# Cross attention and a routed feed-forward block: the transposition of the inputs ahead of the scores, the scaled block product ahead of the final sum

## The chip, the cores and the metric

The kernel runs on one core of one Trainium2 chip. The metric is the device time of one execution in microseconds, as the median of several runs.

## What is computed

The reference, cut to what matters (B = 128 items, T = 128 tokens each, E = 256, H = 16 heads of D = 16, all float32):

```python
x = x + xattn(layernorm(x), ctx)          # Wq, Wkv, Wo, biases
x = x + ffn(layernorm(x))                 # w_router, w_block

def xattn(inp, enc):
    q, k, v = inp @ Wq + bq, enc @ Wk + bk, enc @ Wv + bv     # 16 heads of 16
    scores = einsum('bhqd,bhkd->bhqk', q, k) / sqrt(D)
    attn = softmax(scores, axis=2)        # over the queries
    return einsum('bhqk,bhkd->bhqd', attn, v) @ Wo + bo

def ffn(x):
    top = top_k(x @ w_router, k=96)       # of the 128 tokens of an item
    return x.at[top].set(gelu(x[top] @ w_block))
```

## The kernel before

Each of the five engines runs its own program, written out by hand, and semaphores order them. An item b is one of the 128; the work is a pipeline in which a loop over **slots** `s` runs one stage each for different items. In slot s TensorE makes the scores of item s, transposes the inputs of item s + 5, makes the values of item s - 1, the keys or the queries of a later pair, the projection of item s - 2, the block product (the feed-forward matmul and the router's score) of item s - 4, the transposition of the attention's result of item s - 3, and the attention of item s - 1.

The code below is the program of TensorE for a slot (lines 524 to 541); `settled` or `sure` leaves out waits that the order makes needless:

```python
scores(s)
transpose_inputs(s + 5, s > 2)
values(s - 1)
queries_or_keys(s + 2, 1, sure)
queries_or_keys(s + 3, 0, sure)
...
```

What matters for the change:

- `scores` (line 336, matmuls in line 349) uses the array in four row tiles: 32 rows by 128 columns each. It waits for `recip_23_ready` and `exp_ready[1]` of the item before, which free its PSUM banks.
- `transpose_inputs` (line 361, matmuls in line 378) transposes two halves of `xhat` (the normalised x) and two of `c_sb` (the context) into the bank `ps_t`, with the whole array. From item 10 on it waits for `z_ready` of item b - 10, since `ps_t` also holds the block product: VectorE's `product_scaled` (line 860, operation in line 870) reads that product out of it and raises `z_ready`. So in slot s the transposition waits for the product that VectorE scales in slot s - 1.
- `attention` (line 401, matmuls in line 414) uses the array in four column tiles: 128 rows by 32 columns. It waits for `x1_ready`, which `residual` (line 767, operation in line 773) raises.
- ScalarE takes 16 exponentials with their sums for each item (`exps`, line 593), and between them casts and copies, among them `inputs_high` (line 606), which reads the transposed inputs, and `gelu_tanh` (line 637).
- VectorE's slot (lines 960 to 995) is: `x1_low` (764), four maxima (751) of which the first two wait for the scores, `values_and_bias` (858), `inputs_low` (819), `inverse_sums_01` (811), the queries (832) or the keys (845), `residual` (773), the last maximum, `inverse_sums_23` (804), `final` (923), the statistics of a pair (780 or 797), and `product_scaled` (870). Between them stand the steps of `router`, which finds the 32 dropped tokens of each item for eight items at once. They are spread over slots with s mod 8 of 4, 5, 6, 7 and 0, from s = 12 on. After the third maximum, step 10 (906 and 907) comes where s mod 8 is 0 and step 0 (885) where it is 4. A `max` (896) stands just ahead of `inverse_sums_23` where s mod 8 is 4, 5, 6 or 7. Step 9 (901) comes after the second maximum where s mod 8 is 0.
- GpSimd normalises, scales the values, and does half of the gelu. SyncE issues the DMAs.

An fp32 matmul has two records in the trace, so the 8 matmuls of the scores are 16 rows, the 4 transpositions are 4 rows.

Of the kernel before, what the change touches and what calls it, by code (L numbers as in the profile page):

```python
# [6 lines left out]
def cross_attention_routed_ffn(  # L7
# [40 lines left out]
    with ctx:  # L48
# [81 lines left out]
        def bank(b, j):  # L130
            return J if j == 0 and b % 2 == 1 else j

        def inputs_bank(b):
            return ps_a if b in (1, 3) else ps_t
# [7 lines left out]
        def has(b):  # L142
            return 0 <= b < B

        def upto(b):
            return min(b + 1, B)

        def pair(b):
            return b % R // 2

        def landed(b):
            return b // R * 16 + 16
# [136 lines left out]
        def _(pe):  # L289
# [29 lines left out]
            def pair_ready(b, settled=False):  # L319

                if b % 2 == 0 and has(b):
                    if b == 0:
                        pe.wait_ge(q_raw_ready, upto(b + 1))
                    else:
                        pe.wait_ge(q_eo_in[(b // 2) % 2], stripes(b))
                    if not settled:
                        pe.wait_ge(k_ready, upto(b + 1))

            def inputs_ready(b):

                if has(b):
                    pe.wait_ge(xhat_ready, upto(b))
                    if b % 2 == 0:
                        pe.wait_ge(c_in[pair(b)], landed(b))

            def scores(b):

                if not has(b):
                    return
                r2, h = (b // 2) % 2, b % 2  # L340
                if b == 0:
                    pair_ready(b)
                if has(b - 1):
                    pe.wait_ge(recip_23_ready, upto(b - 1))
                    pe.wait_ge(exp_ready[1], upto(b - 1))
                for c in range(C):
                    for j in range(J):
                        rows = slice(32 * j, 32 * j + 32)
                        mm = nc.tensor.matmul(ps_s[:, bank(b, j), c, :, :], k_sb[rows, r2, c, h * T:(h + 1) * T],  # L349
                                              q_eo[rows, r2, :, c, h, :], start=True, stop=True)  # L350
                        if c == C - 1:
                            mm.then_inc(s_mm[j], 1)
# [8 lines left out]
            def transpose_inputs(b, settled=False):  # L361

                if not has(b):
                    return
                if not settled:
                    inputs_ready(b)
                if has(b - 10):
                    pe.wait_ge(z_ready, upto(b - 10))
                elif 2 <= b <= 4:
                    pe.wait_ge(t_lo_ready, upto(b - 2))  # L370
                elif b > 4:
                    pe.wait_ge(t_lo_ready, upto(b - 1))
                for kind in range(2):
                    for c in range(C):
                        src = (xhat[:, b % 4, c * P:(c + 1) * P] if kind == 0
                               else c_sb[:, b % 8, c * P:(c + 1) * P])
                        n = kind * C + c
                        mm = nc.tensor.transpose(inputs_bank(b)[:, n * T:(n + 1) * T], src, ident[:, :])  # L378
                mm.then_inc(t_mm, 1)
# [17 lines left out]
            def scaled_values_ready(b):  # L397

                pe.wait_ge(v_pad_ready, upto(b))
# [20 lines left out]
            def values(b):  # L420

                if not has(b):
                    return
                if b == 0:
                    pe.wait_ge(w_lo_ready["v"], 1)
                    pe.wait_ge(w_z_ready, 1)
                if b == B - 1:
                    pe.wait_ge(x1_ready, upto(b - 2))
                elif has(b - 1):
                    pe.wait_ge(o_ready, upto(b - 1))  # L430
                n, h = (b // 2) % 4, b % 2
                three_terms(ps_v,
                            lambda a, c: (t_hi, t_lo)[a][:, n, 1, c, h * T:(h + 1) * T],
                            lambda a, c: (w_hi, w_lo)[a]["v"][:, c, :]).then_inc(v_mm, 1)
# [88 lines left out]

            for s in range(2, B - 1):
                sure = 20 <= s < B - 8
                scores(s)
                transpose_inputs(s + 5, s > 2)
                values(s - 1)
                queries_or_keys(s + 2, 1, sure)
                queries_or_keys(s + 3, 0, sure)  # L530
                keep_columns(s - 16)
                candidates(s - 12)
                projection(s - 2, sure)
                pair_ready(s + 1, sure)
                inputs_ready(s + 6)
                block_product(s - 4, sure)
                if sure:
                    scaled_values_ready(s - 1)
                transpose_x1(s - 3, sure)
                router_bank_free(s + 1)  # L540
                attention(s - 1, sure)
# [175 lines left out]
        def _(dve):  # L717
# [82 lines left out]
            def inverse_sums_23(b):  # L800

                if has(b):
                    dve.wait_ge(exp_ready[2], upto(b))
                    nc.vector.reciprocal(recip[:, b % 4, :].rearrange("p (c j q) -> p j c q", c=C, j=J)[:, 2:4, :, :],
                                         ps_s[:, 2:4, :, :, 0]).then_inc(recip_23_ready, 1)
# [54 lines left out]
            def product_scaled(b, settled=False):  # L860

                if has(b):
                    dve.wait_ge(z_mm, upto(b))
                    if not settled:
                        dve.wait_ge(rstd2_ready, upto(b))
                    if b % 2 == 0 and has(b - R):
                        dve.wait_ge(stored[pair(b)], landed(b - R))
                    if b == 0:
                        dve.wait_ge(w_lo_ready["v"], 1)
                    nc.vector.tensor_scalar(z_sb[:, b % R, :], ps_z, rstd2[:, b % R:b % R + 1], None,  # L870
                                            ALU.mult).then_inc(z_ready, 1)
# [37 lines left out]
            def final(b, settled=False):  # L909

                if has(b):
                    if b in U_ON_ACT:
                        dve.wait_ge(u_act_ready, u_on_act(b))
                    else:
                        dve.wait_ge(u_ready, b + 1 - u_on_act(b))
                    if settled:
                        pass
                    elif b < GELU_ON_DVE:
                        dve.wait_ge(gelu_ready, upto(b))
                    else:  # L920
                        dve.wait_ge(gelu_dve_ready, b - GELU_ON_DVE + 1)
                    k, r = b % GROUP, b % R
                    nc.vector.scalar_tensor_tensor(z_sb[:, r, 0:E], z_sb[:, r, 0:E], half_keep[:, (b // GROUP) % 2, k:k + 1],  # L923
                                                   x1_sb[:, r, :], ALU.mult, ALU.add).then_inc(final_ready, 1)
# [35 lines left out]
            for s in range(2, B):  # L960
                sure = 20 <= s < B - 1
                x1_low(s - 4)
                if s == 3:
                    block_weights_low()
                router(s - 13, 2)
                router(s - 14, 4)
                router(s - 15, 6)
                router(s - 16, 8)
                maxima(s, 3)
                maxima(s, 2)  # L970
                router(s - 16, 9)
                values_and_bias(s - 1, sure)
                inputs_low(s + 5)
                inverse_sums_01(s - 1)
                maxima(s, 1)
                queries(s + 3, sure)
                router(s - 16, 10)
                router(s - 12, 0)
                keys(s + 2, sure)
                residual(s - 2, sure)  # L980
                maxima(s, 0)
                if s == B - 1:
                    values_and_bias(B - 1)
                router(s - 12, 1)
                router(s - 13, 3)
                router(s - 14, 5)
                router(s - 15, 7)
                inverse_sums_23(s)
                final(s - 16, sure)
                stats2_of_pair(s - 3)  # L990
                if s >= 4:
                    stats1_of_pair(s + 10)
                product_scaled(s - 4, sure)
                if s < 4:
                    stats1_of_pair(2 * s + 6)

# [258 lines left out]
```

## Time and profile before

| | before |
|---|---|
| median of 3 runs | 900.6 us (900.34 to 901.68) |
| profiled execution, its own time | 898.87 us |
| its span | 897.1 us |
| PE, PEld busy | 97%, 84% |
| DVE, ACT, POOL busy | 95%, 97%, 89% |
| granted TensorE clock, mean | 0.991 |

PE is TensorE's matmuls, PEld its weight loads, DVE is VectorE, ACT ScalarE, POOL GpSimd. The times of matmul ends are modelled. An instruction of ACT that stands in the engine's queue behind another is counted as busy from its issue, so that the duration of one holds its time in the queue. "[0.33 <-DVE z_sb L870]" behind a row says how long the engine was idle before it and what the profile holds to have released it; "issue" means that it shows no releaser.

### The profile page before, as it was taken

To read this page: it belongs to the slowest core of one execution; us is meant where nothing else is said; L and a number is where in the kernel's file an instruction comes from. 1 tells how busy PE (TensorE), PEld (TensorE's weight loads), DVE (VectorE), ACT (ScalarE), POOL (GpSimd) and SP (SyncE) were. 2 spreads that over 40 slices of the span, in tenths; PEclk is the share of its full clock that TensorE was granted. 3 is DMA by queue.
4 is the path that set the end of the run, shared out by engine and by line. 5 is a ranking of instruction groups with operands and counts; after the bars stand their busy time and mean duration, and the time that the engine had idled before them with its cause. 6 is when DMAs were issued, how large, how long until landed. Compare 5 with 4: busy or idle time off the path is not lost. (4 is left out here: it accounts for less than half of the span.)

```text
span 897.1 us, 31627 instructions
## 1 busy us (share of the span) xinstructions
PE 867.0 (97%) x10562; PEld 757.0 (84%) x10562; DVE 852.6 (95%) x2068; ACT 869.5 (97%) x4632; POOL 794.4 (89%) x1488
## 2 busy tenths in 40 slices
PE   7999999999999999999999999999999999999972
PEld 6788888888888888888888888888888888888862
DVE  6898999999999999999999999999999999999987
ACT  5999999999999999999999999999999999999984
POOL 4668889999999999999999999999999999998764
PEclk9999999999999999999999999999999999999996
DMA  6222123233233223233223223323322322311102
GB/s 204 64 65 73 47 63 96 57 88 95 58 88 95 66 83 93 61 88 92 76 74 92 74 77 90 91 61 88 84 69 88 96 59 85 97 46 52 49 25 94
DMA packets 70978, 70.48 MB, mean 79 GB/s; under 512 B 12064, under 2 KB 62752, under 8 KB 70816
## 3 DMA queue, kind: packets, MB, share of 16 engines
q1 hardware_dynamic: 69456, 67.68, 26.3%
q8 instruction: 84, 1.38, 0.6%
q10 hardware_dynamic: 1360, 0.79, 0.3%
q14 instruction: 78, 0.64, 0.2%
HBM read 35.13 MB, written 16.78 MB: 58 GB/s over the span
## 5 line engine op out<-in xcount | busy, mean ns | idle before, releaser
L593 ACT ACTIVATE e_sb<-ps_s,neg_max 128x128 f32<-128x128 f32 x2048 | 776.7, 661 | 2.4 <-DVE neg_max L751 2.1
L593 ACT ACTIVATION_READ_ACCUMULATOR e_sb<-ps_s,neg_max 128x1 f32 x2048 | 735.0, 486 | 0.0
L751 DVE TENSOR_REDUCE neg_max<-ps_s 128x4 f32<-128x512 f32 x512 | 331.7, 668 | 24.0 <-PE ps_s L349 22.5
L349 PE MATMUL ps_s<-q_eo,k_sb 32*128 32x256 f32 x2048 | 146.7, 400 | 1.4 <-ACT e_sb L593 0.6
L414 PE MATMUL ps_a<-e_sb,v_pad 128*32 128x128 f32 x4096 | 138.3, 276 | 2.1 <-POOL v_pad L1086 0.9
L310 PE MATMUL ps_a<-w_o_sb,o_sb 128*128 128x256 f32 x512 | 131.8, 380 | 3.2 <-DVE v_sb L858 3.1
L414 PEld LDWEIGHTS ps_a<-e_sb,v_pad 128*32 128x32 f32 x4096 | 104.1, 110 | 23.7 <-issue 21.3
L349 PEld LDWEIGHTS ps_s<-q_eo,k_sb 32*128 32x128 f32 x2048 | 95.9, 184 | 29.3 <-issue 26.7
L1075 POOL TENSOR_TENSOR x_sb<-x_sb,bo_sb 128x256 f32<-128x256 f32 x128 | 108.9, 852 | 0.3
L1086 POOL TENSOR_TENSOR v_pad<-v_sb,recip 128x256 f32<-128x256 f32 x128 | 79.5, 621 | 27.8 <-DVE recip L811 27.4
L637 ACT ACTIVATE g_sb<-g_sb 128x256 f32<-128x256 f32 x128 | 101.6, 794 | 1.4 <-POOL g_sb L1133 1.4
L606 ACT CAST t_hi<-ps_t 128x512 fp32r<-128x512 f32 x126 | 96.9, 769 | 4.1 <-PE ps_t L378 3.8
L303 PE MATMUL ps_t<-w_z_hi,xt_hi 128*128 128x258 f32 x256 | 96.8, 378 | 2.2 <-DVE z_sb L870 2.2
L310 PEld LDWEIGHTS ps_a<-w_o_sb,o_sb 128*128 128x128 f32 x512 | 88.6, 190 | 10.7 <-issue 3.6
L614 ACT COPY o_sb<-ps_a 128x256 f32<-128x256 f32 x128 | 94.2, 736 | 2.4 <-PE ps_a L414 2.4
L580 ACT CAST xt_hi<-ps_q 128x256 fp32r<-128x256 f32 x128 | 91.3, 713 | 1.4 <-PE ps_q L394 1.4
L1133 POOL TENSOR_TENSOR g_sb<-g_sb,z_sb 128x256 f32<-128x256 f32 x128 | 88.3, 690 | 0.3
L819 DVE TENSOR_TENSOR t_lo<-ps_t,t_hi 128x512 fp32r<-128x512 f32 x126 | 85.3, 677 | 1.1 <-ACT t_hi L606 1.0
L303 PE MATMUL ps_a<-w_v_hi,t_hi 128*128 128x256 f32 x256 | 83.2, 325 | 0.7 <-DVE w_z_sb L743 0.7
L1147 POOL TENSOR_TENSOR z_sb<-g_sb,z_sb 128x256 f32<-128x256 f32 x121 | 83.3, 688 | 0.0
L1116 POOL TENSOR_TENSOR g_sb<-z_sb 128x256 f32<-128x256 f32 x123 | 75.4, 613 | 0.0
L303 PE MATMUL ps_q<-t_hi,w_q_hi 128*128 128x256 f32 x256 | 72.5, 283 | 0.2 <-DVE t_lo L819 0.2
(110 smaller groups left out, 2464.8 us busy)
## 6 DMA issues: line engine op xcount, KB each, us to landing
x_sb<-in_x SPq DMA_DIRECT2D x64, 256.0 KB, 2.9
c_sb<-in_ctx SPq DMA_DIRECT2D x64, 256.0 KB, 3.1
out<-z_sb SPq DMA_DIRECT2D x64, 256.0 KB, 2.4
q_eo<-q_raw SPq DMA_DIRECT2D x504, 32.0 KB, 2.0
z_sb<-in_L_xattn_Wkv ACTq DMA_DIRECT2D x2, 256.0 KB, 7.3
z_sb<-in_L_xattn_Wq ACTq DMA_DIRECT2D x1, 256.0 KB, 4.1
w_z_sb<-in_L_ffn_w_block SPq DMA_DIRECT2D x1, 256.0 KB, 7.8
w_o_sb<-in_L_xattn_Wo SPq DMA_DIRECT2D x1, 256.0 KB, 7.1
```

The source lines that it names most:

```text
L303: last = nc.tensor.matmul(dst, lhs(a, c), rhs(b, c), start=(c == 0 and n == 0), stop=(c == C - 1 and n == len(terms) - 1))
L310: last = nc.tensor.matmul(dst, lhs(c), rhs(c), start=(c == 0), stop=(c == C - 1))
L349: mm = nc.tensor.matmul(ps_s[:, bank(b, j), c, :, :], k_sb[rows, r2, c, h * T:(h + 1) * T], q_eo[rows, r2, :, c, h, :], start=True, stop=True)
L414: mm = nc.tensor.matmul(ps_attn[32 * j:32 * j + 32, c * T:(c + 1) * T], v_pad[:, b % 2, c * J + j, par:par + 2, :].rearrange("p a d -> p ( ...
L580: nc.scalar.copy(xt_hi[:, b % 2, :], ps_xt).then_inc(xt_hi_ready, 1)
L593: last = nc.scalar.activation(e_sb[:, b % 4, j, c, par, :], ps_s[:, bank(b, j), c, par, :], ACT.Exp, bias=neg_max[:, b % 4, h:h + 1], accu ...
L606: nc.scalar.copy(t_hi[:, n, :, :, h * T:(h + 1) * T].rearrange("p k c t -> p (k c) t"), inputs_bank(b)[:, :].rearrange("p (n t) -> p n t", ...
L614: nc.scalar.copy(o_sb[:, b % 2, :], ps_attn).then_inc(o_ready, 1)
L637: nc.scalar.activation(g_sb[:, b % 4, :], g_sb[:, b % 4, :], ACT.Tanh, scale=SLOPE).then_inc(tanh_ready, 1)
L751: nc.vector.tensor_reduce(neg_max[:, b % 4, :].rearrange("p (c j q) -> p j c q", c=C, j=J)[:, j, :, :], ps_s[:, bank(b, j), :, :, :], AX.X ...
L1075: nc.gpsimd.tensor_tensor(x_sb[:, b % R, :], x_sb[:, b % R, :], bo_sb[:, :], ALU.add).then_inc(xb_ready, 1)
L1133: nc.gpsimd.tensor_tensor(g_sb[:, b % 4, :], g_sb[:, b % 4, :], z_sb[:, b % R, 0:E], ALU.mult).then_inc(cubic_ready, 1)
```

## The change

In slots from 4 on TensorE transposes the inputs of item s + 5 ahead of the scores of item s. VectorE scales the block product of item s - 4 just behind `inverse_sums_23`, ahead of `final` and the statistics, and it waits for `rstd2_ready` in every slot (before, slots 20 to 126 left that wait out).

```diff
             for s in range(2, B - 1):
                 sure = 20 <= s < B - 8
+                if s >= 4:
+                    transpose_inputs(s + 5, True)
                 scores(s)
-                transpose_inputs(s + 5, s > 2)
+                if s < 4:
+                    transpose_inputs(s + 5, s > 2)
                 values(s - 1)
                 queries_or_keys(s + 2, 1, sure)
...
                 inverse_sums_23(s)
+                product_scaled(s - 4)
                 final(s - 16, sure)
                 stats2_of_pair(s - 3)
                 if s >= 4:
                     stats1_of_pair(s + 10)
-                product_scaled(s - 4, sure)
                 if s < 4:
                     stats1_of_pair(2 * s + 6)
```

TensorE from the end of one slot into the next, before (`ps_q<-ident,x_sb` is the transposition of the attention's result, `ps_a<-e_sb,v_pad` the attention, `ps_s` the scores, `ps_t<-ident` the transposition of the inputs, `ps_a<-w_v_hi` the values):

```order
L394 MATMUL ps_q<-ident,x_sb 128x128 x2
L414 MATMUL ps_a<-e_sb,v_pad 32x128 x16
L349 MATMUL ps_s<-q_eo,k_sb 128x256 x8
L378 MATMUL ps_t<-ident,xhat 128x128 x2
L378 MATMUL ps_t<-ident,c_sb 128x128 x2
L303 MATMUL ps_a<-w_v_hi,t_hi 128x256
```

and in the changed kernel:

```order
L394 MATMUL ps_q<-ident,x_sb 128x128 x2
L414 MATMUL ps_a<-e_sb,v_pad 32x128 x16
L378 MATMUL ps_t<-ident,xhat 128x128 x2
L378 MATMUL ps_t<-ident,c_sb 128x128 x2
L349 MATMUL ps_s<-q_eo,k_sb 128x256 x8
L303 MATMUL ps_a<-w_v_hi,t_hi 128x256
```

The four transpositions, which use the whole array, now stand between the attention (column tiles) and the scores (row tiles); the scores stand between them and the values.

VectorE at the end of a slot with a router step, before (`recip<-ps_s` is `inverse_sums_23`, `z_sb<-z_sb,half_keep,x_sb` is `final`, `z_sb<-ps_t,rstd` is `product_scaled`):

```order
L751 TENSOR_REDUCE neg_max<-ps_s 128x2x2
L896 MAX top<-cand 8x8
L804 RECIPROCAL recip<-ps_s 128x2x2x2
L923 SCALAR_TENSOR_TENSOR z_sb<-z_sb,half_keep,x_sb 128x256
L797 BN_STATS st<-x_sb 128x6
L870 TENSOR_SCALAR z_sb<-ps_t,rstd 128x258
L764 TENSOR_TENSOR xt_lo<-ps_q,xt_hi 128x256
L890 MATCH_REPLACE cand<-top,cand 8x128
L751 TENSOR_REDUCE neg_max<-ps_s 128x2x2 x2
```

and in the changed kernel (its lines from 526 on stand 3 lower):

```order
L754 TENSOR_REDUCE neg_max<-ps_s 128x2x2
L899 MAX top<-cand 8x8
L807 RECIPROCAL recip<-ps_s 128x2x2x2
L873 TENSOR_SCALAR z_sb<-ps_t,rstd 128x258
L926 SCALAR_TENSOR_TENSOR z_sb<-z_sb,half_keep,x_sb 128x256
L800 BN_STATS st<-x_sb 128x6
L767 TENSOR_TENSOR xt_lo<-ps_q,xt_hi 128x256
L893 MATCH_REPLACE cand<-top,cand 8x128
L754 TENSOR_REDUCE neg_max<-ps_s 128x2x2 x2
```

The scaled product moved up by two places; everything ahead of the reciprocal kept its place.

## Rows read from the trace of the kernel before

**Rows 1.** The page, busy time, share of the span and instructions of each engine

```profile
PE 867.0 (97%) x10562; PEld 757.0 (84%) x10562; DVE 852.6 (95%) x2068; ACT 869.5 (97%) x4632; POOL 794.4 (89%) x1488
```

**Rows 2.** Waits, 150 to 800 us: engine, line, releaser: us in total, times, longest

```profile
PEld ps_t L378 <- DVE z_sb L870: 24.5, 73, 0.6
...
PEld ps_t L378 <- issue: 8.3, 25, 0.3
```

**Rows 3.** Timeline of ACT, slot 66: start, us, engine, line, operation

```profile
458.02 0.81 ACT L606 CAST t_hi<-ps_t 128x512 fp32r<-128x512 f32 x1
```

**Rows 4.** Timeline of ACT, slot 5

```profile
50.84 0.59 ACT L606 CAST t_hi<-ps_t 128x512 fp32r<-128x512 f32 x1
```

**Rows 5.** Timeline of PE, end of slot 65 and start of slot 66

```profile
454.93 0.38 PE L394 MATMUL ps_q<-ident,x_sb 128*128 128x128 f32 x2
455.24 1.08 PE L414 MATMUL ps_a<-e_sb,v_pad 128*32 128x128 f32 x32
456.25 1.15 PE L349 MATMUL ps_s<-q_eo,k_sb 32*128 32x256 f32 x16
457.33 0.44 PE L378 MATMUL ps_t<-ident,xhat 128*128 128x128 f32 x2
457.61 0.38 PE L378 MATMUL ps_t<-ident,c_sb 128*128 128x128 f32 x2
...
457.95 0.28 PE L303 MATMUL ps_a<-w_v_hi,t_lo 128*128 128x256 f32 x1
```

**Rows 6.** Timeline of PE, slot 125, which has no transposition of inputs

```profile
849.77 1.15 PE L349 MATMUL ps_s<-q_eo,k_sb 32*128 32x256 f32 x16
...
851.08 0.28 PE L303 MATMUL ps_a<-w_v_hi,t_lo 128*128 128x256 f32 x1
```

**Rows 7.** Timeline of PE, the scores of slots 5 and 6

```profile
49.08 1.15 PE L349 MATMUL ps_s<-q_eo,k_sb 32*128 32x256 f32 x16
...
55.70 1.15 PE L349 MATMUL ps_s<-q_eo,k_sb 32*128 32x256 f32 x16
```

**Rows 8.** Timelines of DVE and of PEld, slots 119 and 120

```profile
817.53 0.46 DVE L870 TENSOR_SCALAR z_sb<-ps_t,rstd 128x258 f32<-128x258 f32 x1
...
818.04 0.20 PEld L378 LDWEIGHTS ps_t<-ident,xhat 128*128 128x128 f32 x2 [0.46 <-DVE z_sb L870]
```

**Rows 9.** Timeline of DVE, slot 66, without a router step

```profile
457.54 1.29 DVE L751 TENSOR_REDUCE neg_max<-ps_s 128x4 f32<-128x512 f32 x2 [0.31 <-PE ps_s L349]
...
460.35 0.68 DVE L845 TENSOR_TENSOR k_sb<-ps_q,bk_sb 128x512 f32<-128x512 f32 x1
461.04 0.42 DVE L773 TENSOR_TENSOR x_sb<-ps_a,x_sb 128x256 f32<-128x256 f32 x1
...
461.98 0.20 DVE L804 RECIPROCAL recip<-ps_s 128x8 f32<-128x8 f32 x1
462.09 0.43 DVE L923 SCALAR_TENSOR_TENSOR z_sb<-z_sb,half_keep,x_sb 128x256 f32<-128x256 f32 x1
```

**Rows 10.** Timeline of DVE, slots with router steps: 60, 63, 64

```profile
417.46 1.29 DVE L751 TENSOR_REDUCE neg_max<-ps_s 128x4 f32<-128x512 f32 x2
...
422.22 0.18 DVE L804 RECIPROCAL recip<-ps_s 128x8 f32<-128x8 f32 x1
...
437.52 1.27 DVE L751 TENSOR_REDUCE neg_max<-ps_s 128x4 f32<-128x512 f32 x2
...
442.15 0.18 DVE L804 RECIPROCAL recip<-ps_s 128x8 f32<-128x8 f32 x1
...
444.20 1.27 DVE L751 TENSOR_REDUCE neg_max<-ps_s 128x4 f32<-128x512 f32 x2
...
447.28 0.67 DVE L845 TENSOR_TENSOR k_sb<-ps_q,bk_sb 128x512 f32<-128x512 f32 x1
447.87 0.40 DVE L773 TENSOR_TENSOR x_sb<-ps_a,x_sb 128x256 f32<-128x256 f32 x1
...
448.80 0.18 DVE L804 RECIPROCAL recip<-ps_s 128x8 f32<-128x8 f32 x1
```

## The prediction

> **What bounds the kernel now.** I read the page first. Four engines are busy for 89 to 97% of the span [rows 1], so the shares name no bound, and the question is which loop sets the length of a slot. The scores start at 49.08 in slot 5 [rows 7] and at 456.25 in slot 66 [rows 5]: 407.17 us for 61 slots, **6.675 us a slot**.
>
> Then the waits. TensorE seems to lose 24.5 us between 150 and 800 us to transpositions that wait for the scaled product [rows 2]. This is what the change aims at, and the reader should distrust it. The same idle time stands 25 times with no releaser, 8.3 us, and the mean is equal: 24.5 / 73 = 0.34 and 8.3 / 25 = 0.33 us [rows 2]. A wait for another engine would scatter.
>
> The timelines tell why. From the start of the scores to the start of the next group is 457.33 - 456.25 = 1.08 us [rows 5]. In slot 125 the values follow the scores directly, with no transposition between. There the second matmul of the values starts 1.31 us after the scores [rows 6]. So whatever full-array work follows the scores starts late: it is the price of leaving the row tiles, not a wait for a product. A real wait for the product is in slot 120: the product ends at 817.53 + 0.46 = 817.99, the transposition starts at 818.04, 0.05 us later, and the idle time is 0.46 [rows 8].
>
> ScalarE is next. In slot 5 its cast of the transposed inputs takes 0.59 us on an empty queue [rows 4], in slot 66 it takes 0.81 [rows 3]: 0.22 us of other work is still queued ahead of it. ScalarE never runs dry in the steady part, and **it is the bound at 6.675**. TensorE is only just behind it: in slots 5 to 6, where ScalarE's queue is not yet full, the scores come 55.70 - 49.08 = 6.62 us apart [rows 7]. That is TensorE's own length of a slot. An earlier transposition therefore buys almost nothing: a cast that is ready sooner stands longer in a full queue.
>
> **The change, part by part.**
>
> *TensorE's own loop.* Before, from the attention to the second matmul of the values: 457.95 - 455.24 = 2.71 us [rows 5]. After, it is three steps.
> - Attention to transposition: no row has it in the steady part. The bounds are 1.01, the step from attention to scores (456.25 - 455.24) [rows 5], and 0.81, if the 0.20 between tiled modes fell away. I take 1.01, since the next group leaves the column tiles either way.
> - Transposition to scores: the third and fourth transposition have to pass and then comes the first tiled matmul. The nearest row is the pair ahead of the attention, which also goes from the whole array to tiles: 455.24 - 454.93 = 0.31. With the first two transpositions, 457.61 - 457.33 = 0.28, this makes 0.59 [rows 5]. The lower bound is 0.39, if going from the whole array to row tiles cost nothing.
> - Scores to the second matmul of the values: 1.31 [rows 6].
>
> The sum is 2.91, **0.20 us more**; TensorE's loop becomes 6.62 + 0.20 = 6.82. The reason is countable: whole array to column tiles, to row tiles, to whole array were three changes of shape in a slot, and now there are four.
>
> Whether the array really has to stop for transpositions followed by scores no row shows. The Trainium skill says it does: "TensorEngine Tiling (Array Packing)", Key Properties, has it that a change of the tiling mode, though not of the tile within it, drains TensorE. The page speaks against this change; by it the sum stays as it is, and without it the step would be 0.39 and every loop below 0.20 shorter.
>
> *The loop through VectorE.* Before, the scores stood ahead of the transposition and owed nothing to the product. Now they are queued behind a transposition that waits for it, so this ring closes: scores, maxima, VectorE's slot up to the product, transposition, scores.
> - Scores to the first maximum: 457.54 - 456.25 = 1.29 [rows 5, 9].
> - First maximum to the reciprocal ahead of the product: 461.98 - 457.54 = 4.44 [rows 9]. In it the residual waits 0.09 for the projection: it starts 0.69 after the keys [rows 9], and 0.59 to 0.60 where VectorE is late [rows 10]. TensorE reaches the projection earlier relative to the scores, since no transposition lies between, so this wait goes: 4.35.
> - Reciprocal to the end of the product: it starts 0.11 behind, as `final` does now (462.09 - 461.98) [rows 9], and takes 0.46 [rows 8]: 0.57. Bounds: 0.57 and, if it overlapped nothing, 0.20 + 0.46 = 0.66.
> - Product to transposition 0.05 [rows 8], transposition to scores 0.59 as above.
>
> That is 1.29 + 4.35 + 0.57 + 0.05 + 0.59 = **6.85** without a router step, level with TensorE's 6.82. Router steps lie inside the ring and add to it. First maximum to reciprocal is 442.15 - 437.52 = 4.63 in slot 63, less the same 0.09 is 4.54; it is 448.80 - 444.20 = 4.60 in slot 64 and 422.22 - 417.46 = 4.76 in slot 60, where the residual has no wait to give back [rows 10]. So the ring is 7.04 where s mod 8 is 5, 6 or 7, 7.10 at 0 and 7.26 at 4. Eight slots give 3 x 6.85 + 3 x 7.04 + 7.10 + 7.26 = 56.03, a mean of **7.00**.
>
> The first maximum of a slot always waits for that slot's scores, so what one slot loses no later slot makes up.
>
> *The other moves.* `final` and the statistics fall behind the product, by 0.46 us at most, into the time in which VectorE waits for the scores (0.31 even now [rows 9], more afterwards): nothing. If that cover were gone it would be that 0.46 in a slot. The wait for `rstd2_ready` is for a value that GpSimd makes near the start of its slot's work, right after normalising, and what is queued behind it on VectorE is `final`: nothing. SyncE's stores come 0.4 us later with many slots of slack. GpSimd's squares get their product earlier: nothing, as they are not waited for.
>
> *The sum.* Slots 12 to 121 have the router steps: 110 x (7.00 - 6.675) = +35.8 us. The eight slots before: 8 x (6.85 - 6.62) = +1.8. Slot 4 has its scores 0.6 later, and slot 122, whose successor has no transposition, gives 0.6 back. In the last five slots only the product moves: within 0.5. I take off 1.5 us, because the rows are rounded up at each step of the ring and the few late slots of the kernel before fall inside the longer slots. That leaves +36. The profiled execution's own time is 898.87, 1.7 below the median of 900.6; I forecast against the median, **936 us**.
>
> **The rivals.**
> 1. *TensorE alone sets the slot.* The product reaches the transposition in time, because VectorE takes up more slack than I count. For it: the two rings are within 0.03 without a router step. Against it: the router's rows are there in five of eight slots. Time: 118 x (6.82 - 6.675) = +17, 918 us.
> 2. *The change from whole array to row tiles is free.* The rings are 0.20 shorter: 6.675 (ScalarE), 6.84, 6.90 and 7.06, a mean of 6.81. For it: no row shows that step. Against it: all the other changes of shape cost the same. Time: 110 x 0.135 = +15, 915 us.
> 3. *Faster: the gaps on TensorE are waits after all.* Then the early transposition fills the gap ahead of the scores, its own gap goes, and ScalarE's cast is issued sooner; the steady slot falls to the 6.62 of the early slots [rows 7], 118 x -0.055 = -6.5, 894 us. It decides if the gap ahead of the values, now right behind the scores, vanishes. Against it: slot 125 has that gap [rows 6], and the cast shows a queue [rows 3].
> 4. *ScalarE stays the bound at 6.675,* with both rings below it, which needs rivals 1 and 2 at once and more: within 1 us of 900.
>
> **How the numbers follow.** My forecast has 0.71, rival 1 has 0.11, rival 2 has 0.10, rival 3 has 0.04, rival 4 has 0.04. A measurement of this kernel tells about 0.2%, 1.8 us, from no change. Faster is rival 3, 0.04; the same is rival 4, 0.04; slower 0.92. The range reaches up to the forecast with 0.66 for the product and some 0.4 us of contention in a few slots, 944, and down to rival 2, 914; it leaves out rivals 3 and 4 and the ends of the others.
>
> **What would show it.** Right: scores about 6.85 apart in slots without router steps and 7.0 to 7.3 apart in the others; the transposition 0.05 us after the product's end; its start to the scores' start 0.59; the values' second matmul 1.31 after the scores; casts of 0.59 on ScalarE, whose busy share falls. Wrong: an even 6.8 in every slot (rival 1), 0.39 from transposition to scores (rival 2), or a slot of 6.68 or less (rivals 3, 4).

## The result and the profile after

| | before | changed |
|---|---|---|
| median | 900.64 us (4 runs) | 933.88 us (4 runs, 933.64 to 934.69) |
| profiled execution: own time, span | 898.87, 897.1 us | 933.64, 931.8 us |
| slot, mean over slots 24 to 118 | 6.68 us | 6.98 us |

The ratio is 1.0368, with a 95% interval of 1.0355 to 1.038: 33.2 us slower. The two profiled executions are 34.8 us apart, because the one of the kernel before took 1.8 us less than the median beside it. Shares of the loss are therefore taken from the lengths of slots below and not from ratios. The length of a slot is the time between the first matmul of the scores of one slot and that of the next. By s mod 8, as means over slots 24 to 118:

| s mod 8 | 0 | 1 | 2 | 3 | 4 | 5 | 6 | 7 |
|---|---|---|---|---|---|---|---|---|
| before | 6.73 | 6.63 | 6.67 | 6.67 | 6.73 | 6.66 | 6.67 | 6.67 |
| changed | 7.13 | 6.85 | 6.86 | 6.86 | 7.19 | 6.99 | 6.99 | 6.99 |
| forecast | 7.10 | 6.85 | 6.85 | 6.85 | 7.26 | 7.04 | 7.04 | 7.04 |

The page of the changed kernel, busy times and two groups, beside [rows 1]:

```profile
PE 897.2 (96%) x10562; PEld 756.7 (81%) x10562; DVE 856.9 (92%) x2068; ACT 882.6 (95%) x4632; POOL 795.6 (85%) x1488
...
L596 ACT ACTIVATE e_sb<-ps_s,neg_max 128x128 f32<-128x128 f32 x2048 | 740.9, 476 | 24.2 <-DVE neg_max L754 21.3
...
L754 DVE TENSOR_REDUCE neg_max<-ps_s 128x4 f32<-128x512 f32 x512 | 333.2, 672 | 54.8 <-PE ps_s L349 54.7
```

The engines execute as many instructions as before, and ScalarE and VectorE now wait more. ScalarE's exponentials wait 21.3 us for the maxima (2.1 before), the maxima 54.7 us for the scores (22.5 before). The waits between 150 and 800 us, beside [rows 2]:

```profile
DVE neg_max L754 <- PE ps_s L349: 33.1, 93, 0.7
PEld ps_a L303 <- issue: 30.8, 93, 0.3
...
PEld ps_t L378 <- DVE z_sb L873: 25.0, 93, 0.3
```

The row that the change seems to aim at, 25.0 us for the transposition, 0.27 each, is as long as before. And the 0.33 us idle ahead of whatever follows the scores is still there, 30.8 us in 93 slots, now ahead of the values.

TensorE from slot 65 into slot 66 (s mod 8 is 2, no router step), beside [rows 5]:

```profile
473.23 0.41 PE L394 MATMUL ps_q<-ident,x_sb 128*128 128x128 f32 x2
473.57 1.08 PE L414 MATMUL ps_a<-e_sb,v_pad 128*32 128x128 f32 x32
474.58 0.44 PE L378 MATMUL ps_t<-ident,xhat 128*128 128x128 f32 x2
474.85 0.38 PE L378 MATMUL ps_t<-ident,c_sb 128*128 128x128 f32 x2
475.17 1.15 PE L349 MATMUL ps_s<-q_eo,k_sb 32*128 32x256 f32 x16
476.24 0.39 PE L303 MATMUL ps_a<-w_v_hi,t_hi 128*128 128x256 f32 x1
476.47 0.27 PE L303 MATMUL ps_a<-w_v_hi,t_lo 128*128 128x256 f32 x1
```

Attention to transposition is 1.01, transposition to scores 0.59, scores to the second matmul of the values 1.30, together 2.90 where the sum had 2.91. These are the first rows of a step from the whole array to row tiles: 0.59 is 0.28 for the first two transpositions, 0.11 for the third and 0.20 from the fourth to the scores, as it is into the column tiles in [rows 5], 0.31 - 0.11.

VectorE in slot 62, with a router step (s mod 8 is 6), beside [rows 9, 10], and then TensorE's weight loads at its end, beside [rows 8]:

```profile
448.50 1.29 DVE L754 TENSOR_REDUCE neg_max<-ps_s 128x4 f32<-128x512 f32 x2 [0.28 <-PE ps_s L349]
...
452.83 0.27 DVE L899 MAX8 top<-cand 8x8 f32<-8x128 f32 x1
453.03 0.18 DVE L807 RECIPROCAL recip<-ps_s 128x8 f32<-128x8 f32 x1
453.14 0.42 DVE L873 TENSOR_SCALAR z_sb<-ps_t,rstd 128x258 f32<-128x258 f32 x1
```

```profile
453.61 0.20 PEld L378 LDWEIGHTS ps_t<-ident,xhat 128*128 128x128 f32 x2 [0.33 <-DVE z_sb L873]
...
454.20 0.31 PEld L349 LDWEIGHTS ps_s<-q_eo,k_sb 32*128 32x128 f32 x8 [0.17 <-issue]
```

The product ends at 453.14 + 0.42 = 453.56, the transposition starts at 453.61, the scores at 454.20. The scores of this slot began at 447.21, so the ring is closed: 1.29 to the first maximum, 4.53 to the reciprocal, 0.53 to the product's end, 0.05 and 0.59, together 6.99.

In slot 65 it is not closed. There the product ends before the transposition could start anyway (its row on VectorE, same view):

```profile
474.04 0.43 DVE L873 TENSOR_SCALAR z_sb<-ps_t,rstd 128x258 f32<-128x258 f32 x1
```

It ends at 474.47, 0.11 us ahead of the transposition at 474.58, where a transposition that waits starts 0.05 behind it. In the slots without router steps the product is in time by 0.06 us.

What does set the 6.86 of those slots is a second ring through VectorE. TensorE's transposition of the attention's result waits by the code for VectorE's queries or keys of the same slot, whose bank it writes. In all slots from 24 to 118 of the changed kernel its weight load starts 0.11 to 0.12 us behind their end. In the kernel before, the means by s mod 8 are 0.26 to 0.43. VectorE's queries and TensorE's weight load in slot 65 of the kernel before, 0.43 apart:

```profile
453.72 0.68 DVE L832 TENSOR_TENSOR q_raw<-ps_q,bq_sb 128x512 f32<-128x512 f32 x1
```

```profile
454.83 0.25 PEld L394 LDWEIGHTS ps_q<-ident,x_sb 128*128 128x128 f32 x2
```

The ring of the changed kernel is 4.77 from the scores to the end of the queries or keys, 0.12 to the weight load, 0.03 to the transposition of the attention's result, 0.34 to the attention, 1.01 to the transposition of the inputs, 0.59 to the scores: 6.86. The moved transposition has put its 0.59 into this ring as well.

### The profile page after: what moved, and what is told of

The parts are those of the page before. It is cut to its first block and busy times, and to the rows that moved or that the text cites. A ratio compares the mean times of both kernels' runs of the same rounds, so it can differ in the third digit from the quotient of the medians.

```text
span 931.8 us, 31680 instructions
## 1 busy us (share of the span) xinstructions
PE 897.2 (96%) x10562; PEld 756.7 (81%) x10562; DVE 856.9 (92%) x2068; ACT 882.6 (95%) x4632; POOL 795.6 (85%) x1488
## 5 line engine op out<-in xcount | busy, mean ns | idle before, releaser
L596 ACT ACTIVATE e_sb<-ps_s,neg_max 128x128 f32<-128x128 f32 x2048 | 740.9, 476 | 24.2 <-DVE neg_max L754 21.3
L596 ACT ACTIVATION_READ_ACCUMULATOR e_sb<-ps_s,neg_max 128x1 f32 x2048 | 599.5, 300 | 0.0
L754 DVE TENSOR_REDUCE neg_max<-ps_s 128x4 f32<-128x512 f32 x512 | 333.2, 672 | 54.8 <-PE ps_s L349 54.7
L349 PEld LDWEIGHTS ps_s<-q_eo,k_sb 32*128 32x128 f32 x2048 | 92.7, 184 | 26.0 <-issue 21.8
L1136 POOL TENSOR_TENSOR g_sb<-g_sb,z_sb 128x256 f32<-128x256 f32 x128 | 106.7, 834 | 0.3
L1078 POOL TENSOR_TENSOR x_sb<-x_sb,bo_sb 128x256 f32<-128x256 f32 x128 | 96.4, 754 | 0.3
L303 PE MATMUL ps_a<-w_v_hi,t_hi 128*128 128x256 f32 x256 | 85.6, 334 | 0.7 <-DVE w_z_sb L746 0.7
L303 PEld LDWEIGHTS ps_a<-w_v_hi,t_hi 128*128 128x128 f32 x256 | 47.8, 187 | 42.2 <-issue 40.0
L640 ACT ACTIVATE g_sb<-g_sb 128x256 f32<-128x256 f32 x128 | 77.8, 608 | 1.4 <-POOL g_sb L1136 1.4
L926 DVE SCALAR_TENSOR_TENSOR z_sb<-z_sb,half_keep,x_sb 128x256 f32<-128x256 f32 x128 | 75.2, 593 | 1.8 <-POOL x_sb L1168 1.8
L617 ACT COPY o_sb<-ps_a 128x256 f32<-128x256 f32 x128 | 70.5, 551 | 2.4 <-PE ps_a L414 2.4
```

What stands on the lines that cost most here:

```text
L303: last = nc.tensor.matmul(dst, lhs(a, c), rhs(b, c), start=(c == 0 and n == 0), stop=(c == C - 1 and n == len(terms) - 1))
L596: last = nc.scalar.activation(e_sb[:, b % 4, j, c, par, :], ps_s[:, bank(b, j), c, par, :], ACT.Exp, bias=neg_max[:, b % 4, h:h + 1], accu ...
L754: nc.vector.tensor_reduce(neg_max[:, b % 4, :].rearrange("p (c j q) -> p j c q", c=C, j=J)[:, j, :, :], ps_s[:, bank(b, j), :, :, :], AX.X ...
L1078: nc.gpsimd.tensor_tensor(x_sb[:, b % R, :], x_sb[:, b % R, :], bo_sb[:, :], ALU.add).then_inc(xb_ready, 1)
L1136: nc.gpsimd.tensor_tensor(g_sb[:, b % 4, :], g_sb[:, b % 4, :], z_sb[:, b % R, 0:E], ALU.mult).then_inc(cubic_ready, 1)
```

## Experiments

Ratios are to the kernel before on the same chip. The runs of the kernel before there had medians of 898.7 to 899.1 us, where those beside the changed kernel had 900.64. The changed kernel's ratio of 1.0368 is therefore some 0.2% low beside the ratios here.

**TensorE's half alone** is the first hunk of the change, without the second (the scaled product keeps its place behind the statistics).

```diff
+                if s >= 4:
+                    transpose_inputs(s + 5, True)
                 scores(s)
-                transpose_inputs(s + 5, s > 2)
+                if s < 4:
+                    transpose_inputs(s + 5, s > 2)
```

> TensorE's half alone: the transposition ahead of the scores, the scaled product still behind the final sum and the statistics. My theory (the ring scores, maxima, product, transposition, scores): the product ends 1.35 us after the reciprocal in place of 0.35, so a slot without router steps goes from 6.86 to about 7.85 us, and those with them to 8.0 to 8.2; in all about 1040 us. Rival, TensorE's own order and its fourth change of shape set the slot whatever VectorE does: 6.82 a slot, 918 us. Rival, the transposition's gap was a wait that the earlier place hides: below 900 us.

Measured: 1049.6 us, ratio 1.1677 (1.1655 to 1.1698). Slots 7.81 us without router steps, 7.99 with s mod 8 of 5 to 7, 8.07 at 0, 8.68 at 4. VectorE and TensorE at the end of slot 61:

```profile
499.43 0.18 DVE L807 RECIPROCAL recip<-ps_s 128x8 f32<-128x8 f32 x1
...
500.49 0.46 DVE L873 TENSOR_SCALAR z_sb<-ps_t,rstd 128x258 f32<-128x258 f32 x1
```

```profile
501.00 0.44 PE L378 MATMUL ps_t<-ident,xhat 128*128 128x128 f32 x2 [1.06 <-DVE z_sb L873]
...
501.59 1.15 PE L349 MATMUL ps_s<-q_eo,k_sb 32*128 32x256 f32 x16
```

The ring with its product 1 us later: product ends 500.95, transposition 501.00, scores 501.59. Both rivals fall. Outside of s mod 8 = 4 the slot is 0.94 to 1.0 us longer than in the changed kernel, which is what `final` and the statistics take on VectorE between the reciprocal and the product. At 4 it is 1.49 longer: there `final` itself takes longer, 0.93 us in slot 60; why is not shown. The early transposition does much more harm without the early product.

**VectorE's half alone** is the second hunk without the first.

```diff
                 inverse_sums_23(s)
+                product_scaled(s - 4)
                 final(s - 16, sure)
                 stats2_of_pair(s - 3)
                 if s >= 4:
                     stats1_of_pair(s + 10)
-                product_scaled(s - 4, sure)
```

> VectorE's half alone: the product scaled earlier, the transposition behind the scores as before. My theory: ScalarE keeps the slot at 6.675 us and the idle 0.33 us of TensorE ahead of the transposition stays, since it is the change of shape and no wait for the product; 900.6 us, within 1. Rival, that idle time is a wait for the product: it goes, and with it up to 0.055 us a slot, 894 us. Rival, the later final sum and statistics are waited for: slower than 902.

Measured: 898.36 us, ratio 0.9992 (0.9983 to 1.0001), no change. Its waits between 150 and 800 us:

```profile
PEld ps_t L378 <- issue: 32.5, 98, 0.3
```

The product starts 0.11 us behind the reciprocal in place of some 1.08. Counted from the scores it is done 1.03 us earlier in the mean, and 1.2 to 1.5 us ahead of the transposition. The idle time ahead of the transposition is what it was, 32.5 / 98 = 0.33 us. Only its label moved, from "DVE z_sb" to "issue". It was no wait for the product, save in the few slots like 120 where it was longer.

**One extra transposition between attention and scores,** on the kernel before.

```diff
+                if 4 <= b < B - 5:
+                    nc.tensor.transpose(ps_s[:, bank(b, 0), 0, 0, :], ident[:, :], ident[:, :])
                 for c in range(C):
                     for j in range(J):
                         rows = slice(32 * j, 32 * j + 32)
```

> The kernel before with one more transposition of a constant in each slot, between the attention and the scores, so that the whole array stands between column tiles and row tiles. My theory: it costs its 0.11 us and the steps into and out of the whole array, 0.20 in all more than attention to scores directly; TensorE's slot is 6.82, 118 x 0.15 = +17, 918 us. Rival, only the work counts and not the shape: TensorE's slot is 6.62 + 0.11 = 6.73, 118 x 0.055 = +6.5, 907 us.

Measured: 925.6 us, ratio 1.0296 (1.0281 to 1.0312), slots 6.87 to 6.88, and 6.98 at 0 and 4. TensorE into slot 62:

```profile
441.79 1.08 PE L416 MATMUL ps_a<-e_sb,v_pad 128*32 128x128 f32 x32
442.81 0.33 PE L347 MATMUL ps_s<-ident 128*128 128x128 f32 x1
443.06 1.15 PE L351 MATMUL ps_s<-q_eo,k_sb 32*128 32x256 f32 x16
```

Attention to scores is 443.06 - 441.79 = 1.27 where it was 1.01: 0.26 for one transposition, not the 0.20 expected, so 918 us was too low. The first instruction in a new shape is slow as well. The first of the four in [rows 5] steps 0.28 - 0.11 = 0.17 to the second, not 0.11, and a group of one consists of that first instruction. The rival's 0.11 is well off.

**The same transposition inside its own group,** on the kernel before.

```diff
+                if b >= 9:
+                    nc.tensor.transpose(ps_t[:, 0:T], ident[:, :], ident[:, :])
                 for kind in range(2):
                     for c in range(C):
```

> The kernel before with one more transposition of a constant in each slot, just ahead of the four of the inputs and in their shape: 0.11 us of TensorE, no new change of shape. My theory (TensorE's own slot is 6.62 us, 6.73 where s mod 8 is 0 or 4, since the router has one transposition of its own there; ScalarE's is 6.675): 6.73 and 6.84, a mean of 6.76, 118 x 0.08 = +9, about 908 us, a third of what the same transposition cost between attention and scores (925.6). Rival, only the work counts and not the shape: the same 925 as there. Rival, TensorE has real waits of 0.3 us in every slot that absorb it: 899 to 900 us.

Measured: 911.2 us, ratio 1.0134 (1.0119 to 1.015). Slots 6.73 (0.11 more than TensorE's 6.62), 6.83 at 0, but 7.00 at 4 and 6.78 at 5, more than expected. Scores of slots 58 and 59:

```profile
408.36 1.15 PE L349 MATMUL ps_s<-q_eo,k_sb 32*128 32x256 f32 x16
...
415.09 0.93 PE L349 MATMUL ps_s<-q_eo,k_sb 32*128 32x256 f32 x12
```

The slots at 4 and 5 hold real waits for the product. VectorE and TensorE's weight load ahead of slot 60's transpositions:

```profile
421.03 0.98 DVE L925 SCALAR_TENSOR_TENSOR z_sb<-z_sb,half_keep,x_sb 128x256 f32<-128x256 f32 x1
...
422.55 0.46 DVE L872 TENSOR_SCALAR z_sb<-ps_t,rstd 128x258 f32<-128x258 f32 x1
```

```profile
423.07 0.14 PEld L374 LDWEIGHTS ps_t<-ident 128*128 128x128 f32 x1 [0.51 <-DVE z_sb L872]
```

The product ends at 423.01, the transposition's weights load 0.06 later, and the idle time is 0.51 in place of 0.33. `final` (0.98 us, 0.43 in [rows 9]) had delayed the product; what stretched it is not shown.

The same instruction cost 12.4 us inside its group, these waits included, and 26.6 us where it separates two shapes. Of 0.11 us more of TensorE's work a slot, 0.06 shows where no router step stands (6.73 after 6.67), so TensorE was within 0.05 to 0.06 us of being the bound.

**The router's max behind the product,** on the changed kernel.

```diff
-                router(s - 12, 1)
-                router(s - 13, 3)
-                router(s - 14, 5)
-                router(s - 15, 7)
                 inverse_sums_23(s)
                 product_scaled(s - 4)
+                router(s - 12, 1)
+                router(s - 13, 3)
+                router(s - 14, 5)
+                router(s - 15, 7)
```

> The changed kernel with the router's max steps moved from ahead of the reciprocal to behind the scaled product. My theory: the router's steps lie inside the ring, so slots with s mod 8 of 5, 6 and 7 fall from 6.99 to 6.86 us, that of 4 from 7.19 to 7.05, the one of 0 stays at 7.13; 110 x 0.065 = 7 us less than the changed kernel, 927 us. Rival, TensorE alone sets the slot: no change, 934 us.

Measured: 926.6 us, ratio 1.0309 (1.0295 to 1.0323). Slots 6.86 at 5, 6 and 7, 7.04 at 4, 7.12 at 0. TensorE, the scores of slots 61 and 62:

```profile
436.90 1.15 PE L349 MATMUL ps_s<-q_eo,k_sb 32*128 32x256 f32 x16
...
443.76 0.91 PE L349 MATMUL ps_s<-q_eo,k_sb 32*128 32x256 f32 x9
```

An instruction of 0.2 us, moved by two places on VectorE, gives 0.13 us back in each slot where it stood in the ring, on a kernel whose VectorE has 8% idle time. It gave no more than that because the ring through the queries or keys, 6.86, comes next.

**The product still earlier,** ahead of the last maximum, on the changed kernel.

```diff
                 residual(s - 2, sure)
+                product_scaled(s - 4)
                 maxima(s, 0)
...
                 inverse_sums_23(s)
-                product_scaled(s - 4)
```

> The changed kernel with the scaled product ahead of the last maximum, so that it ends about 0.7 us sooner than the transposition needs it. My theory: VectorE's ring lets go in the slots with router steps, and TensorE's own order with its fourth change of shape is left: 6.85 where no router transposition stands on TensorE, at most 7.1 where s mod 8 is 0 or 4, a mean of 6.90; about 925 us where the changed kernel has 932 to 934. Rival, the transposition's wait for the product is all that was lost: back to 6.68 a slot, 900 us.

Measured: 927.1 us, ratio 1.0312 (1.0298 to 1.0326), and slot for slot what the kernel with the max behind the product has: 6.86, 7.04 at 4, 7.12 at 0. VectorE and TensorE in slot 61:

```profile
441.81 0.49 DVE L873 TENSOR_SCALAR z_sb<-ps_t,rstd 128x258 f32<-128x258 f32 x1
```

```profile
442.96 0.44 PE L378 MATMUL ps_t<-ident,xhat 128*128 128x128 f32 x2
```

The product ends at 442.30, 0.66 us before the transposition, which no longer waits for it. The mean slot is 6.91 where the changed kernel has 6.98 and the kernel before 6.68. So **the wait for the product is between a fifth and a quarter of the loss, 0.07 of 0.30 us a slot**, and it exists where s mod 8 is 4 to 7.

The rest is the order on TensorE, but not TensorE alone. VectorE's keys and TensorE's weight load behind them in slot 56 (s mod 8 is 0), then the queries and the weight load in slot 61:

```profile
406.32 0.67 DVE L848 TENSOR_TENSOR k_sb<-ps_q,bk_sb 128x512 f32<-128x512 f32 x1
```

```profile
407.11 0.20 PEld L394 LDWEIGHTS ps_q<-ident,x_sb 128*128 128x128 f32 x2 [0.19 <-issue]
```

```profile
440.78 0.68 DVE L835 TENSOR_TENSOR q_raw<-ps_q,bq_sb 128x512 f32<-128x512 f32 x1
```

```profile
441.57 0.20 PEld L394 LDWEIGHTS ps_q<-ident,x_sb 128*128 128x128 f32 x2
```

The weight load starts 0.12 and 0.11 us behind the queries' or keys' end, in slot 56 after 0.19 us of idle time. This ring gives all three lengths. The queries or keys end 4.77 us after the scores where no router step stands ahead of them, 4.96 at 4 and 5.04 at 0, where one does. With 0.12 + 0.03 + 0.34 + 1.01 + 0.59 = 2.09 that is 6.86, 7.05 and 7.13, for 6.86, 7.04 and 7.12 measured. In slot 61 the weight load shows no idle time of its own. What shows there is the 0.34 to the attention, 0.31 in [rows 5]; whether the late weight load makes it, or the residual, for which the attention waits, stays open. No run takes this ring out. TensorE's own 6.82, and 6.93 with the router's transposition, would make a mean of 6.85, an estimate. By it some 0.17 of the 0.30 us are TensorE's own order, 0.06 to 0.07 this ring, and 0.07 the wait for the product.

**Is TensorE just behind ScalarE?** The forecast rests on 6.675 for ScalarE and 6.62 for TensorE. The test is to shorten ScalarE. On the kernel before, the sums of the exponentials of j = 0 go to PSUM in place of SBUF.

```diff
-                                                    accum_out=(ps_s[:, j, c, par, 0:1] if j >= 2 else
+                                                    accum_out=(ps_s[:, bank(b, j), c, par, 0:1] if j != 1 else
...
+                    halves = recip[:, b % 4, :].rearrange("p (c j q) -> p j c q", c=C, j=J)
+                    nc.vector.reciprocal(halves[:, 1, :, :], sums[:, b % 4, :, 1, :])
+                    nc.vector.reciprocal(halves[:, 0, :, :],
+                                         ps_s[:, bank(b, 0), :, :, 0]).then_inc(recip_ready, 1)
...
-                    pe.wait_ge(exp_ready[0], upto(b + 11))
+                    pe.wait_ge(recip_ready, upto(b + 11))
...
-                    pe.wait_ge(exp_ready[0], upto(b + 15))
+                    pe.wait_ge(recip_ready, upto(b + 15))
```

> The kernel before; the sums of the exponentials of j = 0 go to PSUM (into the bank just read) in place of SBUF, as those of j = 2 and 3 do, and VectorE takes their reciprocals with an instruction of its own. In the trace an exponential with its sum into PSUM is followed by the next after 0.30 us, into SBUF after 0.34. My theory (ScalarE bounds the slot at 6.675 us, TensorE stands at 6.62): ScalarE loses 4 x 0.03 = 0.12 us, and the slot falls to TensorE's 6.62; 118 x 0.055 = -6.5, 894 us. Rival, VectorE's extra 0.11 us binds in the slots with router steps, where it has no idle time: 900 to 904 us.

Measured: 903.7 us, ratio 1.0059 (1.0045 to 1.0072), a miss. The slots say why: 6.62 to 6.64 at 1, 2, 3, 5, 6 and 7, as forecast, but 7.08 at 0 and 6.84 at 4. The number lies in the rival's range, but its reason, VectorE without idle time in router slots, would show at 5, 6 and 7 as well. At 0 and 4 TensorE's transpositions for the router write the bank that now holds the sums, so they wait for VectorE's reciprocal. TensorE's weight loads in slot 56:

```profile
395.25 0.19 PEld L303 LDWEIGHTS ps_q<-t_lo,w_k_hi 128*128 128x128 f32 x1
395.71 0.14 PEld L502 LDWEIGHTS ps_s<-ident,keep_row 128*128 128x128 f32 x1 [0.28 <-issue]
```

A wait that I had added and not priced: the projection, the residual and the attention are all queued behind it on TensorE.

**The same, without those items.** Items whose bank the router writes keep their sums in SBUF, and the two waits are again those of the kernel before.

```diff
+        def sum0_in_psum(b):
+            return 4 <= b < B - 4 and b % 4 != 3
...
-                                                    accum_out=(ps_s[:, j, c, par, 0:1] if j >= 2 else
+                                                    accum_out=(ps_s[:, bank(b, j), c, par, 0:1]
+                                                               if j >= 2 or j == 0 and sum0_in_psum(b) else
```

> The kernel before with the sums of j = 0 in PSUM, but not for the items whose bank the router's transpositions write in the next slot (b mod 4 is 3), which keep the sums in SBUF and the waits of before. My theory: ScalarE's slot falls below TensorE's, and TensorE's stays: 6.63 a slot, 6.73 where s mod 8 is 0 or 4, a mean of 6.655 for 6.679; 118 x -0.024 = -3, about 896 us where before has 899. Rival, VectorE's extra reciprocal holds the slots with router steps: no gain or a loss, 899 to 901.

Measured: 896.5 us, ratio 0.9974 (0.9963 to 0.9984): **0.3% faster than the kernel before**, a small gain, but clear of the noise. Slots 6.62 to 6.64, 6.73 at 4, 6.75 at 0, mean 6.66. ScalarE and TensorE in slot 59:

```profile
411.08 0.59 ACT L610 CAST t_hi<-ps_t 128x512 fp32r<-128x512 f32 x1
```

```profile
409.31 1.15 PE L352 MATMUL ps_s<-q_eo,k_sb 32*128 32x256 f32 x16
...
415.94 0.50 PE L352 MATMUL ps_s<-q_eo,k_sb 32*128 32x256 f32 x4
```

The cast takes 0.59, as in [rows 4] and not 0.81 as in [rows 3]: ScalarE's queue runs empty once a slot, and the scores are 415.94 - 409.31 = 6.63 apart. With ScalarE shortened TensorE is the bound, at 0.05 us less than ScalarE had in the kernel before, as the forecast had it.

## Why the prediction was right

**The bound before, 6.675 on ScalarE with 6.62 on TensorE: right.** Shown from both sides, by the extra transposition in its own group (6.62 + 0.11 = 6.73 appears) and by the shorter ScalarE (TensorE's 6.62 to 6.64 appear).

**The idle time ahead of the transposition is no wait for the product: right.** VectorE's half alone makes the product 1.0 us earlier and leaves the 0.33 us where it was. One of the arguments was weak, though: that a wait would scatter. In the changed kernel the transposition is idle for 0.33 us in one router slot after another where it waits for the product, and for 0.20 where it does not, because a ring repeats itself. The experiment decides this, not the evenness.

**TensorE's loop, 6.62 + 0.20 = 6.82: right in its terms, and never the bound.** 2.90 for 2.91 measured. But no slot of the changed kernel is 6.82 long. The prediction closed one ring through VectorE, by way of the product, and left out the other, by way of the queries or keys. Before, TensorE came to the transposition of the attention's result late enough for them. With the transposition of the inputs gone from between scores and values it comes there 0.4 us sooner, and waits. That the slots without router steps were forecast at 6.85 and came out at 6.85 to 6.86 is luck: the ring through the product, from which the 6.85 came, does not bind there.

**The ring through VectorE and the product, 7.04 and 7.26 at 5 to 7 and at 4: right, and slightly long.** Where it binds (4 to 7) it is 7.19 at 4 and 6.99 at 5, 6 and 7. Its terms at 5 to 7: 1.29 for 1.29, 4.53 for 4.54, 0.53 for 0.57, 0.05 for 0.05, 0.59 for 0.59. The term that was off is the product's duration: 0.42 us behind a busy VectorE, where the sum had 0.46. At 0 the 7.10 for 7.13 measured is luck again. The slot keeps its 7.12 with the product out of play, since the router steps 9 and 10 delay the keys and TensorE waits for those.

**The split was not forecast.** The forecast took the ring through the product for everything above TensorE's 6.82, some 19 of its 36 us. It makes 0.07 us of a slot's 0.30, 7.4 us over slots 12 to 121. Rival 1, TensorE alone at 918, is no nearer: with the product out of play the kernel still takes 927.1 us, because of the ring through the queries or keys. The two errors, the one ring overrated and the other left out, nearly cancel in the total.

**The casts: wrong.** The forecast expected 0.59 on ScalarE as the sign that it no longer bounds. The cast is 0.79. It is now issued 0.30 us behind the tanh, which takes 0.62. The queue runs dry one instruction later, at the exponential (0.37), which waits for the maximum. ScalarE in slot 66 of the changed kernel:

```profile
476.33 0.79 ACT L609 CAST t_hi<-ps_t 128x512 fp32r<-128x512 f32 x1
477.18 0.37 ACT L596 ACTIVATE e_sb<-ps_s,neg_max 128x128 f32<-128x128 f32 x1
```

**The sum.** Between the two profiled executions, slots 12 to 121 give +33.2 us where the sum had +35.8, slots 4 to 11 give +1.8 for +1.8, the first four +0.4 and the last ones -0.7. That is the 34.8 us between these executions, where the sum had 36. The measured medians are 33.2 us apart, 1.6 less, because the kernel before ran 1.8 us above its profiled execution there. The mean slot was 6.98 for 7.00.

**The rivals.** The free step from whole array to row tiles falls with the 0.59 in the rows after and with the pair of extra transpositions. Faster and unchanged fall with the result.

## What to carry to other kernels

The releaser that a profile names for an idle time is inferred. Look at the same idle time in a slot in which the supposed producer was early, or make the producer early: here the product came 1.0 us sooner and the 0.33 us stayed. Before moving a step on TensorE, count the changes of array shape in the loop before and after; here one more of them cost 0.2 us in a slot of 6.7, and the wait that the move was after was not there to be gained. And when a step moves ahead of another, write down every ring that closes through it, not only the one through the step's own producer, and every instruction that lies inside, also the short ones. An engine's idle share says nothing of what they cost.

## What the runs showed that I had not expected

- In this trace the first instruction in a new array shape steps 0.17 us to the next where the others step 0.11. A lone transposition between column tiles and row tiles costs 0.26 us, one of the same size inside its group 0.11.
- The changed kernel waits for VectorE at a place that the change does not touch: TensorE's transposition of the attention's result, behind the queries or keys.
- Where the sum of an exponential goes changes ScalarE's pace. In the trace of the kernel before, exponentials with their sums in PSUM start 0.30 us apart, those with sums in SBUF 0.34 to 0.35 apart. Moving a quarter of the sums from SBUF to PSUM for three items in four was enough to take ScalarE off the bound. Two exponentials of each kind from slot 65 of the kernel before (sums in PSUM, then in SBUF):

```profile
452.19 0.55 ACT L593 ACTIVATE e_sb<-ps_s,neg_max 128x128 f32<-128x128 f32 x1
...
452.49 0.57 ACT L593 ACTIVATE e_sb<-ps_s,neg_max 128x128 f32<-128x128 f32 x1
...
454.63 0.69 ACT L593 ACTIVATE e_sb<-ps_s,neg_max 128x128 f32<-128x128 f32 x1
...
454.98 0.69 ACT L593 ACTIVATE e_sb<-ps_s,neg_max 128x128 f32<-128x128 f32 x1
```

- The median of the kernel before was 900.6 us in the first runs and 898.7 to 899.1 in those beside the experiments, 0.2% apart, so that small effects are read from ratios to the kernel before in the same session, or from lengths of slots.
